# Graph network in one kernel: the first sweep's rows scaled by VectorE, and the coupled sweep in turns of five blocks

## The reference

```python
h = jax.nn.relu(edge_feat @ W1 + b1)              # layer 4: two hidden layers with silu
w = (h @ W2 + b2).reshape(e, 4, MUL, MUL)
m0 = ALPHA * (jnp.einsum('ei,eio->eo', s_e * sh0[:, None], w_000) + C110 * jnp.einsum('eim,em,eio->eo', v_e, sh1, w_110))
m1 = ALPHA * (jnp.einsum('ei,em,eio->eom', s_e, sh1, w_011) + jnp.einsum('eim,eio->eom', v_e * sh0[:, None, None], w_101))
out0 = jax.ops.segment_sum(m0, dst, num_segments=n)
```

```python
for idx, (le, ln, lo) in enumerate(COMBOS):
    base = jnp.einsum('ijk,ei,emj->emk', CG[le, ln, lo], sh[le], feats[ln])
    msg[lo] = msg[lo] + jnp.einsum('io,eik->eok', W[idx], base)
agg0 = jax.ops.segment_sum(msg[0].reshape(E, M), tgt, num_segments=N)
```

## Time and profile before

| | |
|---|---|
| time, median of 3 runs | 18837.07 us (18817.78 to 18853.27) |
| the profiled execution's own time | 18865.37 us |
| its span, first to last instruction | 18863.6 us |
| busy share of TensorE, VectorE, POOL, ScalarE | 76%, 74%, 53%, 22% |
| mean granted TensorE clock | 0.754 |
| first weighted sweep, from its first to its last add | 80 to 4497 us |
| coupled sweep, POOL's gathers | 4672 to 8944 us |
| last weighted sweep, from its first to its last add | 14707 to 18692 us |

### The profile page before, as it was taken

How to read it: one execution, slowest core, us unless ns; L and a number is a source line. 1 busy time by engine, 2 the same in 40 slices (tenths; PEclk the granted TensorE clock), 3 DMA queues, 4 the chain that set the end, 5 groups by cost and what they waited for, 6 DMA issues and landing times. The chain is left out here.

```text
span 18863.6 us, 319178 instructions
## 1 busy us (share of the span) xinstructions
PE 14294.0 (76%) x90270; PEld 10545.9 (56%) x90270; DVE 13979.9 (74%) x35607; ACT 4058.3 (22%) x9245; POOL 9929.0 (53%) x9721
## 2 busy tenths in 40 slices
PE   8999999998666666666433337776777899999998
PEld 5666666665666666666322235555555555555555
DVE  7787788875333333333899999995999899999996
ACT  2332333332000000000100014443444222222222
POOL 6666666763777777777122210000000677777774
PEclk7777777876555555555555569997999999999998
DMA  1111111111111111111000003331333111111111
GB/s 34 25 25 25 25 25 25 26 25 17 16 16 16 16 16 16 16 16 16 8 1 1 1 32 132 134 133 63 132 134 116 19 18 18 18 18 18 18 18 15
DMA packets 997582, 680.36 MB, mean 36 GB/s; under 512 B 744566, under 2 KB 912467, under 8 KB 997044
## 3 DMA queue, kind: packets, MB, share of 16 engines
q1 hardware_dynamic: 694830, 524.39, 9.5%
q0 software_dynamic: 302720, 155.60, 5.9%
HBM read 669.41 MB, written 9.60 MB: 36 GB/s over the span
## 5 line engine op out<-in xcount | busy, mean ns | idle before, releaser
L526 PE MATMUL weighted_weights_ps<-weighted_w_out,weighted_hidden 128*128 128x256 f32 x12600 | 4127.7, 457 | 530.9 <-DVE weighted_to_s L665 478.6
L734 PE MATMUL coupled_win<-coupled_onehot,coupled_prod 128*125 128x64 f32 x12560 | 2763.8, 418 | 1533.6 <-DVE coupled_prod L770 1533.6
L356 POOL DMA_INDIRECT coupled_rows<-x_after_weighted,coupled_idx x3140 | 3307.2, 1053 | 1164.1 <-issue 954.8
L526 PEld LDWEIGHTS weighted_weights_ps<-weighted_w_out,weighted_hidden 128*128 128x128 f32 x12600 | 2451.6, 215 | 2539.9 <-issue 1698.0
L356 POOL DMA_INDIRECT weighted_rows<-in_x,weighted_idx x3140 | 3068.7, 977 | 1402.9 <-issue 920.0
L734 PEld LDWEIGHTS coupled_win<-coupled_onehot,coupled_prod 128*125 128x125 f32 x12560 | 2678.9, 329 | 1618.5 <-issue 834.8
L356 POOL DMA_INDIRECT weighted_rows<-x_after_convolved,weighted_idx x3140 | 3031.2, 965 | 1043.6 <-issue 940.9
L660 DVE TENSOR_TENSOR weighted_v_v<-weighted_weights_ps,weighted_scaled 128x320 f32<-128x320 f32 x3768 | 1964.5, 576 | 885.3 <-ACT weighted_scaled L587 885.3
L1198 DVE TENSOR_SCALAR cells_to_dst<-from,cells_current 128x224 bf16<-128x224 bf16 x12500 | 2389.7, 273 | 17.9
L1154 PE MATMUL cells_sum_ps<-cells_to_dst,cells_rows 128*96 128x224 bf16 x12500 | 1698.7, 267 | 691.6 <-DVE cells_to_dst L1198 691.6
L559 PEld LDWEIGHTS weighted_win_ps<-weighted_onehot,weighted_prod 128*128 128x128 f32 x12560 | 1833.4, 215 | 100.9
(11 more groups left out here) (203 smaller groups left out, 14930.0 us busy)
## 6 DMA issues: line engine op xcount, KB each, us to landing
cells_src<-cell_sources SPq DMA_DIRECT2D x500, 800.0 KB, 4.1
weighted_feat<-in_ef SPq DMA_DIRECT2D x635, 80.0 KB
weighted_rows<-in_x,weighted_idx POOLq DMA_INDIRECT x3140
coupled_rows<-x_after_weighted,coupled_idx POOLq DMA_INDIRECT x3140, 2.4
weighted_rows<-x_after_convolved,weighted_idx POOLq DMA_INDIRECT x3140
weighted_idx<-in_src_blocks SPq DMA_DIRECT2D x1264, 2.5 KB
weighted_sh<-in_sh SPq DMA_DIRECT2D x1264, 10.0 KB
coupled_sh<-in_sh SPq DMA_DIRECT2D x632, 22.5 KB, 1.7
```

Of the source, the lines that this page charges most:

```text
L356: pool.indirect_dma_start(rows[s][:, t, :], None, table, bass.IndirectOffsetOnAxis(ap=idx[s][:, t:t + 1].bitcast(U32), axis=0))\
L526: mm = pe.matmul(banks[bank][:, t * WPATHS:(t + 1) * WPATHS], hidden[slot][:, t * P:(t + 1) * P], w_out[:, :], start=True, stop=True)
L734: mm = pe.matmul(win_ps[s % 2][0:OCH, c * WINDOW:(c + 1) * WINDOW], prod[s][:, t, c * OCH:(c + 1) * OCH], onehot[s][:, t, :], start=(t == ...
```

## The change

It has two parts. In the first weighted sweep the rows are now scaled as in the last one: ScalarE's `scale_rows` is gone, and VectorE's multiply (L644 before, L633 after) is issued in both sweeps. The function's other instructions stay as they are.

The coupled sweep gets its own loops in turns of `DEEP = 5` blocks: five slots of every array, five PSUM banks for windows (one for each slot), and 125 turns (`ROUNDS`), which is 625 blocks with no padding. VectorE adds a block's window `LAG = 4` blocks later, where it was one. TensorE doesn't wait for adds any more (`summed`), only for the products (`msg_ready`): the add of block n-5 stands ahead of the products of block n in VectorE's stream. The five window positions are loaded behind the first block's products. The four windows that are left at the end are added behind the loop, and at the beginning four windows of zeros are added at a position behind the last node.

```diff
+DEEP = 5
+LAG = 4
+ROUNDS = REAL_BLOCKS // DEEP
...
-                def scale_rows(g, s):
-                    act.wait_ge(gathered[s], g * (16 * TILES) + 16 * TILES)
-                    act.wait_ge(loaded[s], g * 32 + 32)
-                    act.wait_ge(w_used, g * SLOTS + s + 1)
-                    for t in range(TILES):
-                        last = nc.scalar.activation(scaled_pair[s % 2][:, t, MUL:], rows[s][:, t, :], ACT.Copy,
-                                                    scale=sh[s][:, t, 0:1])
-                    last.then_inc(rows_scaled, 1)
...
-                        if not deep:
-                            scale_rows(g, s)
                         block_act(g * SLOTS + s + 3, (s + 3) % SLOTS)
...
-                            if deep:
-                                dve.tensor_tensor(scaled[:, :, MUL:], x[:, :, :],
-                                                  h[:, :, 0:1].broadcast_to([P, TILES, FEAT]), ALU.mult)\
-                                    .then_inc(rows_scaled, 1)
+                            dve.tensor_tensor(scaled[:, :, MUL:], x[:, :, :],
+                                              h[:, :, 0:1].broadcast_to([P, TILES, FEAT]), ALU.mult)\
+                               .then_inc(rows_scaled, 1)
...
+                with sp.Fori(0, passes, 1) as p:
+                    with sp.Fori(0, ROUNDS, 1) as i:
+                        for s in range(DEEP):
+                            sp.wait_ge(msg_ready, (p * ROUNDS + i) * DEEP + s + 1)
+                            fill(s, i * DEEP + (DEEP + s))
...
+                pe.sem_inc(spread, LAG)
+                pe.wait_ge(ones, ONES)
+                with pe.Fori(0, passes * ROUNDS, 1) as g:
+                    for s in range(DEEP):
+                        pe.wait_ge(msg_ready, g * DEEP + s + 1)
                         for c in range(2):
                             for t in range(TILES):
-                                mm = pe.matmul(win_ps[s % 2][0:OCH, c * WINDOW:(c + 1) * WINDOW],
+                                mm = pe.matmul(win_ps[s][0:OCH, c * WINDOW:(c + 1) * WINDOW],
...
+                    dve.memset(win_ps[s][:, 0:2 * WINDOW], 0.0).then_inc(ones, 1)
...
-                            if s > 0:
-                                add_window(n - 1, s - 1, bases[s - 1])
-                        add_window(g * SLOTS + (SLOTS - 1), SLOTS - 1, bases[SLOTS - 1])
+                            if s == 0:
+                                bases = win.bases(i * DEEP, DEEP)
+                            add_window(n + 1, n + p * LAG, (s - LAG) % DEEP, bases[s])
+                    last = win.bases(REAL_BLOCKS, LAG)
+                    for j in range(LAG):
+                        add_window((p + 1) * REAL_BLOCKS + j + 1, (p + 1) * REAL_BLOCKS + p * LAG + j,
+                                   (j - LAG) % DEEP, last[j])
```

73 lines of the change are left out of this document (39 added, 34 removed).

## The result

The changed kernel took 18388.4 us (median; 18315.2 to 18407.7), the kernel before 18845.2 us beside it: ratio 0.9747, 95% interval [0.9727, 0.9767]. On the 18837.07 us of the prediction that is 18361 us, 476 us less, where 361 us less and at least 18380 us had been forecast. The direction was right, and POOL is the first sweep's bound, as forecast; the gain was larger than the range allowed.

What follows compares the result with a forecast made beforehand. POOL's gathers were taken as the first sweep's floor, with a loop over TensorE, VectorE and ScalarE and TensorE's clock holding it above. First sweep -341 us, coupled sweep -20 us, together -361 us from 18837 us: 18475 us, range 18380 to 18740 us.

Steps and rivals of the forecast that it cites:

- The wait for ScalarE goes: First sweep: VectorE's wait for ScalarE's five L587, 882 us in all, 1.40 us per block, would disappear.
- POOL is the floor: First sweep: POOL's five gathers set the shortest possible block, 6.35 us, 0.68 us below the 7.03 us before.
- The multiply costs nothing: First sweep: VectorE's added multiply makes its block 5.85 us, below 6.35 us; otherwise it would cost 144 us.
- The rival with gathers lengthened in the first sweep: First sweep: each multiply blocks a gather for 0.32 us, floor 6.67 us, total 18591 us; chance 0.08.
- the middle of 6.35 and 6.6, 6.49 us: First sweep: forecast block period between POOL's floor and a slower estimate, giving 4076 us against 4417 us, 341 us less.
- Way (c): First sweep: with POOL as bound, slack lasts 2.65 blocks at full clock; 5.8 blocks in 38 us, 6.57 us per block.
- The slack argument: First sweep: TensorE has 3.65 us slack, shrinking 0.88 us per block, so some 4.1 full-clock blocks (20.6 us) without a wait.
- Two signs named in advance: First sweep: full-clock stretches over 20 us; wrong if clock stays at 0.77 or below with TensorE's waits as large.
- it is wrong if the coupled period moves from 6.80 us: Coupled sweep: a sign that 3125 gathers stay at 1.36 us each, 6.80 us per block.
- The rival on the other side: First sweep: TensorE's waits grow to 1.38 us per block, clock falls after 6.8 us; about 19390 us total; chance 0.05.
- lag, banks and slot at nothing: Coupled sweep: these are covered by POOL's work and worth nothing; only three fewer padded blocks count, 20 us less.
- The rule weighed in the prediction: First sweep: two-SBUF-input VectorE multiply contends with GpSimd reads; by it the floor would rise by the whole 0.32 us.

## Why the prediction was right, and where it missed

**The wait for ScalarE goes.** Right: 882 us gone, none in its place. But most of it was not on TensorE's path: in the trace of the kernel before some 656 of the 882 us lie in half-clock stretches, in which TensorE stood idle for 1 us in all, and 226 us at full clock. The account of it also named one link too few. It put the blame on TensorE's second L516 of block n+2, behind which VectorE begins late. With that dependence put back the wait was 0.16 us per block; with the five L587 kept and the dependence gone it was 200.2 / 628 = 0.32 us; with both it was 1.40 us.

**POOL is the floor.** Right, and it carried more than the prediction gave it: 6.32 us per block against the 6.35 us worked out, and the kernel with four gathers of five shows that nothing else held the sweep there.

**The multiply costs nothing.** Right. VectorE's block without a wait was put at 5.85 us and is at most 5.79 us, below the floor. The kernel that kept the scaling on ScalarE took 6.34 us per block, no less than the 6.36 us of the one with the multiply on VectorE. The rival with gathers lengthened in the first sweep fell: 959 ns, from 977 ns.

**The term that was mis-sized: the first sweep's period, "the middle of 6.35 and 6.6, 6.49 us".** Measured 6.325 us, 445 us in place of 341 us. Of the 104 us, 88 us are the averaging (6.49 to 6.35) and the rest the floor itself. The middle of 6.35 and 6.6 is also 6.475 and not 6.49, a slip of 9 us. Way (c), which pulled the middle up, took 22.7 us at full clock and then 15.35 us at half, the mean of two stretches of the earlier trace rows. Neither came: most full-clock stretches stayed at 13.7 us, and of the half-clock ones 160 of 173 took 3.4 or 6.8 us. The floor was the right answer, and to average it with a way that no row of before showed was the mistake.

**The slack argument.** Wrong. It said that TensorE would run 4.1 blocks at full clock before it waits. TensorE in the changed kernel, after the clock rose at 2515.7 us:

```profile
2517.01 1.13 PE L529 MATMUL weighted_weights_ps<-weighted_w_out,weighted_hidden 128*128 128x256 f32 x4
...
2523.00 1.10 PE L529 MATMUL weighted_weights_ps<-weighted_w_out,weighted_hidden 128*128 128x256 f32 x4 [0.96 <-DVE weighted_to_s L654]
...
2529.11 1.85 PE L529 MATMUL weighted_weights_ps<-weighted_w_out,weighted_hidden 128*128 128x256 f32 x4 [1.10 <-DVE weighted_to_s L654]
```

The wait stands in the second block, as it did in the earlier trace rows, and the clock falls about where the second such wait ends. The argument let VectorE catch up in each half-clock stretch, "whatever it owed", and then begin a block as soon as its weights are ready. It can't, since POOL now gives it rows just in time: in that same stretch VectorE began its blocks late for them.

```profile
2519.50 0.32 DVE L632 TENSOR_TENSOR weighted_vsh<-weighted_rows,weighted_sh 128x120 f32<-128x120 f32 x1 [0.52 <-DMA weighted_rows<-in_x,weighted_idx]
...
2525.65 0.28 DVE L632 TENSOR_TENSOR weighted_vsh<-weighted_rows,weighted_sh 128x120 f32<-128x120 f32 x1 [0.26 <-DMA weighted_rows<-in_x,weighted_idx]
```

The 0.1 us that the argument gave to the signals was not the fault: from the end of L665 to the matmul that had waited for it the trace of the kernel before has 0.15 us. The kernel with four gathers of five fits the account by rows: with rows earlier its full-clock stretches reached 54.6 and 71.7 us. Two signs named in advance failed with the argument (full-clock stretches over 20 us, which 128 of 172 were not; fewer waits of TensorE). Two more missed narrowly: the add's period of 6.325 us lies under its 6.35 to 6.6, and the gathers of 959 ns under their 965 to 980. The clock over 0.80 and POOL's wait for loads came as forecast. The prediction had also said that it is wrong if the coupled period moves from 6.80 us, and it moved to 6.73. Why the half-clock stretches got shorter was not isolated. In the stretches shown TensorE is without a gap there, 23.90 of 23.9 us before and 6.90 of 6.90 us after. TensorE's wait for VectorE, on which the prediction had built, doesn't tell the clock: its sum over the first sweep is 289 to 365 us in all seven kernels of the sets at 18800 us. What the runs show is only that the clock is 0.77 in the kernel before, 0.85 to 0.87 in the five kernels on POOL's floor and 0.96 where POOL's floor was lowered.

**The rival on the other side.** "The clock falls earlier since POOL's pace makes TensorE's waits longer" did not happen; the waits are 0.96 and 1.10 us, near the 0.99 us of before.

**The coupled sweep, "lag, banks and slot at nothing".** Forecast 20 us less, measured 68 us. The three padded blocks gave their 20 us. Of the rest, some 9 us are waits of POOL for loads, which are gone, and some 39 us are shorter gathers, 1041 for 1053 ns. VectorE's and POOL's timelines in the changed kernel, two blocks:

```profile
6507.96 0.83 DVE L772 TENSOR_TENSOR coupled_prod<-coupled_sh,coupled_rows 128x640 f32<-128x640 f32 x1 [4.79 <-DMA coupled_rows<-x_after_weighted,coupled_idx]
6508.70 0.78 DVE L776 TENSOR_TENSOR coupled_prod<-coupled_sh,coupled_rows 128x600 f32<-128x600 f32 x1
...
6514.99 0.83 DVE L772 TENSOR_TENSOR coupled_prod<-coupled_sh,coupled_rows 128x640 f32<-128x640 f32 x1 [4.92 <-DMA coupled_rows<-x_after_weighted,coupled_idx]
6515.74 0.78 DVE L776 TENSOR_TENSOR coupled_prod<-coupled_sh,coupled_rows 128x600 f32<-128x600 f32 x1
```

```profile
6508.03 1.56 POOL L724 DMA_INDIRECT coupled_rows<-x_after_weighted,coupled_idx  x1 [0.30 <-issue]
6509.90 0.99 POOL L724 DMA_INDIRECT coupled_rows<-x_after_weighted,coupled_idx  x1 [0.30 <-issue]
...
6514.95 0.94 POOL L724 DMA_INDIRECT coupled_rows<-x_after_weighted,coupled_idx  x1 [0.30 <-issue]
6516.19 1.14 POOL L724 DMA_INDIRECT coupled_rows<-x_after_weighted,coupled_idx  x1 [0.30 <-issue]
```

A gather that starts just after L772 does takes 1.56 us and the next 0.99 us, 0.67 us more than two of 0.94; one that starts just before it takes 0.94 us and the next, which starts under L776, 1.14 us, 0.20 us more. Both held gathers end 0.8 us after the end of the product under which they started. Counted over the sweep, gathers above 1.3 us are 601 of 3140 in the kernel before and 594 and 607 in the two kernels that keep its coupled sweep, but 427, 457 and 461 of 3125 in the three that change it. In the kernel before and in the changed one each of these long gathers started while one of the two products ran, and ended 0.81 to 0.83 us after that product's end. In both kernels about one gather per block is held, 623 and 624 in all; but before only 22 of them, and after 195, start near the end of the second product and so take no more than 1.3 us. So the change shifted when the products meet the gathers. Which of the slots, the lag and the later base loads did that was not told apart. That the meeting itself is the cost is shown: with one SBUF input 1065 gathers started under a product and none of them was held, the long gathers are gone, 0 of 3125, and 302 us with them. I had this cost in view for the first sweep, and priced it at nothing in the sweep whose rows showed it.

The rule weighed in the prediction (the Trainium skill, page SBUF — State Buffer, section "Who interferes with whom") says that a VectorE instruction with two SBUF inputs contends with GpSimd's reads of SBUF. It says too that the one that comes second is fully blocked. The trace agrees with both in the coupled sweep: a gather that starts under a product is held until that product has ended, and takes another 0.81 to 0.83 us. It is held for one product and not for both, so the two, some 1.5 us together, lengthen a gather by at most 0.65 us. A gather that starts no more than 0.04 us after a product does isn't held at all. The size that the prediction took from the rule, the whole 0.32 us of the new multiply on each block, was not seen in the first sweep: gathers there got shorter, 959 ns for 977.

## What to carry to other kernels

When the floor of an engine is read from rows, and the change takes away the only long wait that keeps the sweep off it, forecast the floor; a middle between it and a way that no row shows loses the difference. Read which instructions stand behind a dependence on an in-order engine before you move them: here it did as well to issue them one place earlier. And where a sweep is bound by gathers, look at their single durations and not at the mean: two lengths side by side (0.94 and 1.5 us) point to a contention. Here one operand moved to PSUM was worth four times what the whole coupled rewrite was.

## What the runs showed of the hardware that I had not expected

A gather that starts more than 0.04 us into a VectorE product with both inputs in SBUF waits for the end of that product and takes the same time after it, to within 0.02 us: all 601 gathers above 1.3 us of the kernel before and all 427 of the changed one end 0.81 to 0.83 us after it. In a sweep in which the products have one input in PSUM 3119 of 3125 gathers take less than 0.96 us and the longest 1.24 us, where gathers beside products with both in SBUF take up to 1.60 us.

The same kernel takes 18794 to 18845 us in some sets and 22079 to 22535 us, 17 to 20% more, in others, with TensorE's matmuls 1.4 to 2.8 us apart and no wait to show for it; there the changed kernel with the wait put back gained 0.8 to 1.3%. One chip number stands in both groups.

The half-clock stretches of TensorE in the first sweep went mostly from 23.9 and 6.8 us to 6.8 and 3.4 us, with TensorE waiting about 1 us per full-clock block in both kernels.
